# Expert tiles in the order of the token groups, gates in the payload rows, answers added to the output by GpSimd's DMAs

## What is computed

```
xt = layernorm(x2)
p = softmax(xt @ Wr + br);  the two largest of p, divided by their sum, are the gates
h_e = layernorm(relu(xt @ W1[e] + b1[e]), g1[e], be1[e])        # 512 wide
y_e = layernorm(relu(h_e @ W2[e] + b2[e]), g2[e], be2[e])       # 128 wide
out = x2 + sum over the token's two experts of gate * y_e
```

## Time and profile before

| | |
|---|---|
| median of 3 runs | 324.54 us (324.42 to 325.09) |
| the profiled execution, its own time | 327.99 us |
| its span, first to last instruction | 326.2 us |
| mean granted TensorE clock | 0.872 of full speed |
| busy share of the span: PE / DVE / ACT / POOL | 82% / 73% / 67% / 52% |

### The profile page before, as it was taken

How to read it: one execution, slowest core, us unless ns; L and a number is a source line. 1 busy time by engine, 2 the same in 40 slices (tenths; PEclk the granted TensorE clock), 3 DMA queues, 4 the chain that set the end, 5 groups by cost and what they waited for, 6 DMA issues and landing times.

```text
span 326.2 us, 10267 instructions
## 1 busy us (share of the span) xinstructions
PE 266.7 (82%) x2946; PEld 210.5 (65%) x2946; DVE 237.0 (73%) x1076; ACT 219.6 (67%) x750; POOL 169.8 (52%) x282
## 2 busy tenths in 40 slices
PE   3996878749492829558879779999999989999994
PEld 3454667436272513357768669999999979995231
DVE  1789665817482878447788679999999979998046
ACT  2466557355354886265668669999999979988173
POOL 9314755715354457700475556666666656666200
PEclk9999575955768567959999999999999999999999
DMA  6994942113111312530122222222222222211498
GB/s 188 351 290 141 287 149 84 45 52 97 35 57 49 113 42 75 142 100 12 36 59 60 61 58 68 77 70 69 67 72 79 70 59 61 75 44 36 139 348 310
DMA packets 34067, 34.46 MB, mean 106 GB/s; under 512 B 5254, under 2 KB 26086, under 8 KB 34011
## 3 DMA queue, kind: packets, MB, share of 16 engines
q1 hardware_dynamic: 28540, 24.64, 25.6%
q0 software_dynamic: 4320, 8.89, 8.1%
q10 hardware_dynamic: 1152, 0.27, 0.4%
HBM read 19.71 MB, written 11.98 MB: 97 GB/s over the span
## 4 chain that ended last, share of the span: by engine, by line
PE 46%; DVE 12%; another core or an unknown queue 12%; ACT 9%; issue 9%; DMA 5%; SPq 2%; POOL 2%; DVEq 1%; ACTq 1%; POOLq 0%
PE bank L654 22%; PE bank L658 21%; DMA w2f<-answers 2%; ACT ex L1104 2%; SPq L535 2%; PE bank L940 2%; DVE w1f L1548 1%; DVE w2f L1558 1%; POOL answers L638 1%; DVE kq L1741 1%; DMA wr<-in_L_ffn_Wr 1%; ACT xT L1051 1%; ACT w1l L1142 1%; DMA answers<-vo,kb_room 1%
## 5 line engine op out<-in xcount | busy, mean ns | idle before, releaser
L620 POOL DMA_INDIRECT slot_rows<-pay,pos x64 | 65.5, 1024 | 52.3 <-DVE pos L1513 35.0
L638 POOL DMA_INDIRECT answers<-vo,kb_room x66 | 68.8, 1042 | 25.3 <-ACT sd L1284 21.3
L654 PE MATMUL bank<-xsT,w1h 128*128 128x128 f16 x568 | 56.3, 221 | 3.0 <-issue 2.3
L1270 ACT ACTIVATE rh<-bank 128x512 f16<-128x512 f32 x71 | 42.3, 596 | 22.8 <-remote 11.3
L658 PE MATMUL bank<-w2h,rh 128*128 x284 | 52.6, 222 | 5.8 <-ACT w2l L1051 4.3
L658 PE MATMUL bank<-rh 128*128 128x129 f16 x284 | 52.7, 222 | 1.6 <-issue 1.6
L658 PE MATMUL bank<-w2l,rh 128*128 x284 | 52.7, 221 | 1.2 <-issue 1.2
L654 PE MATMUL bank<-xsT,w1l 128*128 128x128 f16 x284 | 52.1, 221 | 0.5 <-issue 0.5
L1741 DVE SCALAR_TENSOR_TENSOR kq<-bank,rh 128x512 f16<-128x512 f32 x71 | 47.9, 675 | 0.1
L654 PEld LDWEIGHTS bank<-xsT,w1h 128*128 x568 | 42.9, 98 | 6.9 <-issue 5.3
L658 PE MATMUL bank<-w2h,kq 128*128 x284 | 40.2, 221 | 2.2 <-DVE kq L1741 2.0
(11 more groups left out here) (255 smaller groups left out, 649.5 us busy)
## 6 DMA issues: line engine op xcount, KB each, us to landing
kb_room<-slot_rows SPq DMA_DIRECT2D x66, 64.5 KB
x_tok<-in_x SPq DMA_DIRECT2D x8, 256.0 KB, 6.9
w1f<-in_L_ffn_W SPq DMA_DIRECT2D x2, 1024.0 KB, 9.3
pay<-pay SPq DMA_DIRECT2D x8, 256.0 KB
w1f<-answers SPq DMA_DIRECT2D x8, 256.0 KB, 5.8
w2f<-answers SPq DMA_DIRECT2D x8, 256.0 KB, 6.7
answers<-vo,kb_room POOLq DMA_INDIRECT x66
w2h<-in_L_ffn_W SPq DMA_DIRECT2D x4, 256.0 KB, 8.1
```

Source lines behind the costliest of these rows:

```text
L620: eng.indirect_dma_start(slots, bass.IndirectOffsetOnAxis(ap=pos[:, g % 2, k, i:i + 1], axis=0), pay[g % 2][:, k, i, :], None).then_inc(s_ ...
L638: eng.indirect_dma_start(answers, bass.IndirectOffsetOnAxis(ap=xs[j % NX][:, 2 * D:2 * D + 2].bitcast(U32), axis=0), z[j % NZ], None).then ...
L654: return eng.matmul(dst, lhsT, rhs, start=start, stop=stop)
L1270: eng.activation(rh_all(j), psH[j % 3][:, :].rearrange("p (c n) -> p c n", c=FC), ACT.Relu).then_inc(s_rh, 1)
```

## The change

- **Tile order.** AHEAD becomes 4 and WHOLE 24. The tiles after them are laid out in levels: the whole tiles of the groups up to 5, up to 6, up to 7 and up to 8 (LEVELS = 6, RUNS = 48 runs in place of 16), so that a tile holds rows of a bounded set of groups. TensorE counts the rows for the levels (`rows_by`, four more small matmuls per group), VectorE's tables get wider. `group_done(g)` is the tile after which all rows of group g have been answered: 39 for g up to 3, then 47, 55, 63 and 71. `whole_places` and `words(0)` move one or two groups ahead, and SP issues the first 12 row loads before the payload copy of group 7.
- **Gates in the rows.** A payload row grows by 4 bytes (ROW 258 to 260 halves) and carries its gate. Per group: `gate_diff` and `gate_rows` on VectorE (four small instructions), `gate_exp` on ScalarE; the exponential for all groups before the first tile goes. In each tile step VectorE gets a ninth instruction, `gate_share(p-4)`, between `affine` and `square_sums`, which multiplies 1/sd by the row's gate; ScalarE's `scaled` waits for it.
- **The output.** SP stores x2 to the output during tiles 12 to 19. TensorE forms the offsets among the tiles: transposes of the shares beside tiles 12 to 14, and 16 fp32 products of 256 columns (`offset_sums`) beside `turn(j)`, j = 18, 20, ..., 48; ScalarE copies them to SBUF. GpSimd then issues 24 accumulating DMAs of 256 KB: 8 of offsets into the output at the tile steps 21, 25, ..., 49; 16 from `answers` into the output, both in DRAM, two for each group. The second of a pair waits until the first has landed. Pairs of groups 0 to 4 stand at steps 45 to 54, group 5's at 61 and 62, group 6's at 69 and 70, group 7's behind the loop. The whole end of the kernel before (loads of `answers`, scaling, sums, stores) goes.
- **Payload.** The four late payload scatters stand at steps 2, 5, 8 and 11. The DMAs of payload rows are declared as 32-bit words instead of fp16.

```diff
-    AHEAD = GROUPS - 2
+    AHEAD = GROUPS // 2
...
-    ROW = 2 * D + 2
+    LEVELS = GROUPS - AHEAD + 2
+    RUNS = LEVELS * E
+    ROW = 2 * D + 4
@@ sync
             for g in range(GROUPS):
+                if g == GROUPS - 1:
+                    eng.wait_ge(p_score, GROUPS)
+                    eng.wait_ge(s_tab, 1)
+                    for n in range(2):
+                        eng.wait_ge(s_sc[n], scattered(AHEAD - 2 + n))
+                    for j in range(NX):
+                        tile_rows(j)
...
+                if j < NX + GROUPS:
+                    g = j - NX
+                    for b in range(2):
+                        eng.dma_start(out_v[:, 2 * g + b, :, :], pairs(group(x2, g))[:, b, :, 0:D]).then_inc(s_xout, 16)
-            for g in range(GROUPS):
-                for k in range(K):
-                    eng.dma_start(ya[g][:, k, :, :], ans_v[:, k, g * GT:(g + 1) * GT, :]).then_inc(s_ya[g][k], 16)
@@ gpsimd
+            def offsets_added(g):
+                eng.wait_ge(s_off, 2 * (g + 1))
+                eng.wait_ge(s_xout, 16 * 2 * GROUPS)
+                eng.dma_start(out_v[:, 2 * g:2 * g + 2, :, :], pairs(offsets[g]), accum_op=ALU.add).then_inc(s_sum[g], 16)
+
+            def answers_added(g, k):
+                eng.wait_ge(s_sum[g], 16 * (1 + k))
+                done = min(group_done(g), SLOT_TILES)
+                for j in range(done - NZ, done):
+                    eng.wait_ge(s_ans[j % NZ], answered(j))
+                eng.dma_start(out_flat[g], ans_v[k, g], accum_op=ALU.add, max_dma_last_dim=8192).then_inc(s_sum[g], 16)
+
+            offset_at = {OFFSET_TILES[2 * g + 1] + 1: g for g in range(GROUPS)}
+            for g in range(GROUPS - 1):
+                at = max(at, group_done(g) + 6)
...
             for p in range(SLOT_TILES + 4):
...
-                if p % 4 == 0 and 1 <= p // 4 <= GT:
-                    payload_out(GROUPS - 1, 1, p // 4 - 1)
+                if p % 3 == 2 and p // 3 < GT:
+                    payload_out(GROUPS - 1, 1, p // 3)
+                if p in offset_at:
+                    offsets_added(offset_at[p])
+                if p in answers_at:
+                    answers_added(*answers_at[p])
+            for k in range(K):
+                answers_added(GROUPS - 1, k)
@@ tensor
+            def offset_sums(j):
+                n = OFFSET_TILES.index(j)
+                g, h = n // 2, n % 2
...
+                return mm(beside(j)[:, 0:2 * D], shareT[:, g * P:(g + 1) * P], be2_diag[:, h * 2 * D:(h + 1) * 2 * D])
@@ vector
+            def gate_share(j):
+                eng.wait_ge(s_rs, rooted(j + LAG2))
+                if j >= 4:
+                    eng.wait_ge(s_z, j - 3)
+                eng.tensor_tensor(rg[j % 4][:, :], rs2(j), xs[j % NX][:, 2 * D + 2:2 * D + 4].bitcast(F32), ALU.mult
+                                  ).then_inc(s_rg, 1)
```

More of the change, by code:

```diff
@@ L222, in build @@
         u, ur = ([cxT[:, n * D:(n + 1) * D] for n in range(at, at + 3)] for at in (0, 3))
+        rg = [sb(f"rg_{n}", [P, 1]) for n in range(4)]
         st2 = [sb(f"st2_{n}", [P, 6]) for n in range(4)]
@@ L473, in sync, with rows_of, tile_rows @@
             eng.wait_ge(s_const, 1)
-            eng.dma_start(slots[E * REGION:, :].rearrange("(n p) r -> p n r", p=P), zero_rows[:, E:, :]
+            eng.dma_start(slots[E * REGION:, :].rearrange("(n p) r -> p n r", p=P), zero_rows[:, E:, :].bitcast(U32)
                           ).then_inc(s_zero, 16)
-            for g in range(GROUPS):
+            def rows_of(regs, table, first, least, most):
+                n = min(len(regs), table.shape[1] - first)
+                eng.load(regs[0:n], table[0:1, first:first + n])
+                return [eng.snap(r, min_val=least, max_val=most) for r in regs[0:n]]
+            regs = [eng.alloc_register(f"row{n}") for n in range(2 * E)]
+            rows = []
+            def tile_rows(j):
+                if j % E == 0:
+                    half_regs = regs[j // E % 2 * E:(j // E % 2 + 1) * E]
+                    table = row_tab[:, 0:WHOLE] if j < WHOLE else row_tab[:, :]
+                    rows[:] = rows_of(half_regs, table, j, 0, E * REGION + (SPARE - 1) * P)
+                eng.dma_start(xs[j % NX][:, :].bitcast(U32), slots[bass.ds(rows[j % E], P), :]).then_inc(s_row[j % NX], 16)
+            for g in range(GROUPS):
+                if g == GROUPS - 1:
[5 more added lines that the diff above has]
+                        tile_rows(j)
                 if g in (3, 5):
@@ L496, in sync @@
                               ).then_inc(ld_g2, 16)
-            def rows_of(regs, table, first, least, most):
-                n = min(len(regs), table.shape[1] - first)
-                eng.load(regs[0:n], table[0:1, first:first + n])
-                return [eng.snap(r, min_val=least, max_val=most) for r in regs[0:n]]
[L504 to L509, removed]
-                eng.wait_ge(s_sc[n], scattered(AHEAD - 2 + n))
-            for j in range(SLOT_TILES):
+            for j in range(NX, SLOT_TILES):
                 if j == NX:
                     eng.wait_ge(s_tail, 1)
-                    tails = rows_of(regs[0:E], tail[:, :], 0, 0, (E - 1) * REGION + TOKENS)
+                    tails = rows_of(regs[0:E] if NX // E % 2 else regs[E:], tail[:, :], 0, 0, (E - 1) * REGION + TOKENS)
                     for e_ in range(E):
-                        eng.dma_start(slots[bass.ds(tails[e_], P), :], zero_rows[:, e_, :]).then_inc(s_zero, 16)
+                        eng.dma_start(slots[bass.ds(tails[e_], P), :], zero_rows[:, e_, :].bitcast(U32)).then_inc(s_zero, 16)
                 if j == WHOLE:
@@ L919, in tensor @@
                 if n == 7:
+                    places(0)
                     up_low(1)
```

271 lines of the change are left out of this document (131 added, 140 removed).

## The result

The changed kernel took 362.5 us (median of 4 runs, 359.2 to 365.97) beside 324.81 us for the kernel before in the same job: a ratio of 1.1112 with a 95% interval of [1.1017, 1.1207], some 36 us slower by the ratio. The profiled execution had 362.12 us of its own and a span of 360.4 us, against 327.99 and 326.2, so the span grew by 34.2.

The account below looks back on a forecast made before the run. TensorE and VectorE were taken as full at 1.95 us a tile, with vv allowed 0.33 us late. Terms of 2.5-2.7-2.5-12.1+8.4+1.8+16+35 gave +46.4, on the median 324.54 making 371 us, range 328 to 400.

Parts of the forecast that it names:

- the two largest terms: Tile loop: GpSimd's answer DMAs at +35 us and offset DMAs at +16 us.
- the first rival: Tile loop: each DMA costs only vv's lateness beyond 0.33 us slack, plus pair waits; sum +18.4, 343 us; chance 25%.
- the main case: Whole kernel: each new DMA in the loop costs the full hit; +46.4, 371 us, own range 355 to 388; chance 50%.
- the signs that the forecast named: Late vv at steps 21 to 49, residuals 4.5 us apart, steps 45 to 54 at 4.4 each, first transposes at 132.
- The granted clock, named as a sign against: Tile loop: a granted clock below 1.00 would show the forecast wrong; longer TensorE stalls could bring it; no size given.
- Group stage and early rows: Before the tiles: small added instructions cost +2.5 us; an earlier row table and row loads gain -2.7.
- Payload: First tile steps: of four payload scatters, the one at step 2 is hidden and three still hit; -2.5 us.
- Products: TensorE in the tile loop: 16 offset products at 0.53 us each, +8.4 us; ScalarE's copies lie beside them.
- VectorE's ninth instruction: Each tile step: one more VectorE instruction, taken at 0.04 us for some 45 tiles; +1.8 us.
- Offset DMAs: GpSimd, eight single steps: 2.5 us per hit less 0.5 of slack; +16 us.
- Answer DMAs in the loop: GpSimd, seven pairs at neighbouring steps: 14 at 2.5 us each, no wait for a landing; +35 us.
- Tail: End of the kernel: 20.75 us go, two accumulating DMAs in series of 8.6 us remain; -12.1 us.

Follow-up runs that it names:

- run 9: Kernel before with its four late payload scatters issued ahead of the tile loop, on the third chip: 324.67 us, ratio 0.9873.
- run 10: As run 9, with the row table two groups earlier and the first twelve row loads before the last payload copy: 322.73 us, 0.9834 of the kernel before.
- run 7: Changed kernel without TensorE's 16 offset products, copies and DMAs kept: 357.85 us, against 361.33 with them.
- run 8: Kernel before plus four direct accumulating DMAs of 256 KB from SBUF at steps 28, 34, 40 and 46: 327.05 us, ratio 1.0033.
- run 11: Kernel before plus four indirect scatters of 128 payload rows at steps 28, 34, 40 and 46: 338.15 us, ratio 1.0312.
- run 6: Changed kernel with the same answer DMAs, but no two of a group at neighbouring steps: 342.16 us, 1.0505 of the kernel before.
- run 1: Kernel before with GpSimd also waiting for the last output store, so that it finishes last: 299.61 us, ratio 1.0231.
- run 12: Changed kernel with the final waits for the accumulating DMAs on SP instead of GpSimd: 361.35 us, 1.0998 of the kernel before.

## Why the prediction was right, and where its terms were not

The forecast was slower, 371 us in a range of 328 to 400; it is 362.5. The direction was right, and so were the places: the time is lost where GpSimd's new DMAs hold up vv, above all at the steps 45 to 54. The mechanism of the two largest terms was not. Both took 2 to 2.5 us for every issue and no wait for a landing, and the runs show 0.3 to 0.5 us for an issue beside the other work of the loop and a wait in every pair. That is the mechanism of the first rival, "the hits cost their lateness only" (25%, 343 us). The measured time lies nearer to 371 than to 343 by luck: GpSimd's closing of 8 us, which no case had, stands in for part of what the main case took too much. With the 8.8 us of the tail added, the rival would have come to 352 us and the main case to 380.

Of the signs that the forecast named, the waits behind the offset DMAs are there, but with residuals 2.87 us apart and not 4.5. The steps 45 to 54 take 4.0 us in the mean, as 5.79, 2.47, 4.39 and 3.75 in turn and not 4.4 each. The first transposes are not at 132 us. The last data lands about 9 us behind the last answer, as forecast, but the span ends 8 to 9 us later still. The granted clock, named as a sign against, did fall.

**Group stage and early rows (forecast +2.5 and -2.7; measured about -1).** The first twelve row loads were issued at 126.55 instead of 132.58, but the first transposes stood at 135.24 and not at 132: TensorE no longer waits for them, and would not have come sooner. The first residual is 2.84 us earlier, and 1.81 of these are given back by tile 5. Runs 9 and 10 give theirs back by then too.

**Payload (-2.5; measured near it).** The first of the four scatters of before was not a full hit, as the forecast read it: its tile takes 4.33 us, and 2.99 in run 9 without it. The hit at tile 19 is gone, which shows as -1.29 for tiles 15 to 19, since the products lengthen these four by 1.2 (9.02 against 4 x 1.95). Tiles 11 and 14 still show hits, residuals 4.34 and 4.77 us apart.

**Products (+8.4; measured about +10).** Full TensorE time, as forecast, 2.27 us a tile instead of 1.95: 0.33 for 31 tiles. But ScalarE's copies, costed at nothing because they lie beside the products, are not free: run 7 leaves 0.28 us every second tile. ScalarE's 4.9 idle us in 60 are 0.16 in a tile, and the copy takes 0.41.

**VectorE's ninth instruction (+1.8; measured none).** Tiles with nothing else in them take 1.92 to 1.94 us, as before. There the bound of the tile is TensorE's.

**Offset DMAs (+16; measured 2 to 3).** This is the step that failed. Four tiles are 9.4 us with one and 9.1 without, 0.3 each; six of them in tiles 19 to 47 make the 2 us that the products leave of the 11.24. The forecast took a payload scatter's 2.5 us for a direct DMA, which holds GpSimd as long, and it does: vv ended 1.6 us behind the end of the answer before it (218.11 + 1.03 to 220.00 + 0.78), as beside the scatter (1.5 us). What it doesn't do is break up TensorE's stream, which is two thirds of the scatter's price (runs 8 and 11). The rows of before had said so: from 168.74 to `roots` at 170.10 are 1.36 us, 0.8 more than in the plain tile, and from there to the next residual at 173.27 are 3.17 instead of 1.36. The larger part of the hit lay behind the late instruction, where lateness no longer explains it. The first rival had this right and put the eight at 2 us.

**Answer DMAs in the loop (+35; measured about 28).** Nearly the right size for the wrong reason. The forecast was 2.5 us per issue and no wait; it is about 0.5 per issue and a wait for the landing, 3.4 to 5.0 us from the end of the issue where 3.0 had been taken. Tiles 47 to 70 and the last pair behind them are 18.68 + 6.11 + 3.25 = 28.0 us longer, the last two offset DMAs and some products among them. The parts can be read from the trace, to a us or two: GpSimd's seven waits in the loop are 17.1 us (20.6 less 3.5 of the tail), fourteen issues at 0.5 are 7, and the lower clock gives at least 3.4 more (below). Run 6 shows that it is the wait and what follows from it: the same number of DMAs, 19.2 us less. The Trainium skill, page "DMA: Bandwidth & Descriptors", section "Rules for kernel authors", says to issue early and wait late; run 6 agrees with it. The estimate of 2.6 us by that page's fixed time and rate was too low: 3.4 to 3.6 us in the trace, and more behind another DMA.

**Tail (-12.1; measured -3.3, and +3.25 ahead of it that belong to the last pair).** Two DMAs in series were costed well: from the end of the last scatter, 341.58, the forecast's 1.35 + 8.6 gives 351.5, and data movement stops just before 352. The term lacks what follows, 8 to 9 us in which nothing moves, 7.83 of them GpSimd's DRAIN. Run 1 shows it in the kernel before with nothing else changed, and run 12 that it starts at GpSimd's last instruction. The earlier trace rows don't show it, as GpSimd's queue had ended long before, but the trace of before had it to read: the instructions at the line of the program's end, with a DRAIN of 9.06 us for GpSimd and of 0.007 us for SP.

**Clock.** The one thing that the forecast named against itself did happen: 0.88 from 257 to 298 us, where TensorE idles for 31% of the time, and four stretches at half the clock. The pairs' price holds that. Two of the stretches reach over tiles without a DMA and so show it apart: tiles 58 and 59 take 2.71 and 2.61 us, tiles 66 and 67 take 2.55 and 3.23, where 1.94 is usual, 1.4 and 1.9 us more. What the other two cost is mixed with the waits there. In run 6, with no such waits in the loop, the clock stays at 1.00 there.

Together, against the forecast: offset DMAs -13.5, pairs with their clock -7, ninth instruction -1.8, start -0.8, products +1.6, tail +8.8, and 0.5 that tiles 5 to 15 took more. That is -12.2, from the forecast's +46.4 to the span's +34.2.

## What to carry to other kernels

Before you price an interruption by an event in the trace, split the event: how much lies ahead of the instruction that came late, and how much behind it, and whether the new interruption shares both parts. An accumulating DMA issued from an engine in the loop cost 0.3 to 1.1 us here, while one that had to wait for its predecessor cost its whole landing, and then a slower TensorE behind it; put the dependent ones as far apart as the buffers allow. And look at which engine's queue ends last: moving the last work to GpSimd adds its closing, 6 to 9 us here, so keep the end on another queue. The closing of an engine can be read in the trace even where it is hidden.

## What the runs showed of the hardware

- With GpSimd's queue last, 8.1 us (run 12) to 8.9 us (run 1) pass between the last instruction or store and the end of the span; with SP's last, 2.3 us. GpSimd's DRAIN takes 6.5 us in run 1, 7.8 in the changed kernel, 8.7 in run 12 and 9.1, hidden, in the kernel before.
- A direct DMA from SBUF is shown with 1.36 to 1.37 us on GpSimd, but the next instruction starts 0.8 to 0.9 us behind its start and then takes 0.77 to 0.85 us instead of 0.24. One from DRAM to DRAM, where none stands ahead of it, is shown with 0.8 to 0.96 us, and the next starts 0.6 us behind its start and takes 0.5 to 0.6. An accumulating one of 256 KB from DRAM to DRAM lands 3.4 to 3.6 us after the end of its issue, and 4.9 to 5.0 us where another of 256 KB was issued just ahead.
- TensorE at the granted clock of 0.50 ran 22 instructions in 2 us, at 1.00 it ran 39. The clock fell four times in the loop of the changed kernel, each time after a wait of a pair, and never in that of run 6 behind 181.6 us until its tiles thin out at 314.7.
- An indirect scatter of 128 payload rows beside a full TensorE, in a step that has an answer's scatter too, comes with single matmuls 0.6 to 0.76 us apart and costs 2.5 to 2.6 us on two chips, and 0.8 us on a third. The first part of the program differs too: the tiles start at 118 us on that chip and at 142 on the others, 24 of the 32 us between 293.4 and 325.4. The cause of neither was found.
